# Transposing the heads' outputs on VectorE and placing the squares with 16 on-chip transfers a tile

## The reference

```python
qkv = shift_token(x) @ wqkv                    # 8 heads of 64
q, k, v = (to_heads(t) for t in jnp.split(qkv, 3, axis=-1))
q, k = rotary_xpos(l2norm(q) * qs, l2norm(k) * ksc)
o = local_attention(q, k, v)                   # windows of 64, looking one window back
o = o.transpose(0, 2, 1, 3).reshape(b, n, INNER)   # INNER = 512
x = x + o @ wo
a, g = jnp.split(layernorm(shift_token(x)) @ w1 + b1, 2, axis=-1)
x = x + (a * gelu(g)) @ w2 + b2
```

## Time and profile before

| | |
|---|---|
| median of three runs | 3070.92 us |
| the profiled execution | 3069.8 us |
| its span in the profile | 3068.0 us |
| TensorE (PE) busy | 2989.9 us, 97% |
| VectorE (DVE) busy | 2589.6 us, 84% |
| ScalarE (ACT) busy | 2090.5 us, 68% |
| GpSimd (POOL) busy | 1746.9 us, 57% |
| DMA packets of the hardware queue | 311106 |

### The profile page before, as it was taken

How to read it: one execution, slowest core, us unless ns; L and a number is a source line. 1 busy time by engine, 2 the same in 40 slices (tenths; PEclk the granted TensorE clock), 3 DMA queues, 4 the chain that set the end, 5 groups by cost and what they waited for, 6 DMA issues and landing times.

```text
span 3068.0 us, 84550 instructions
## 1 busy us (share of the span) xinstructions
PE 2989.9 (97%) x30773; PEld 2157.2 (70%) x30773; DVE 2589.6 (84%) x5526; ACT 2090.5 (68%) x5016; POOL 1746.9 (57%) x1158
## 2 busy tenths in 40 slices
PE   7999999999999999989999699999999999999999
PEld 4777777667777777657777477777766677777765
DVE  7999998678888888869999599999966888888866
ACT  4777777437777777328889377777753677777732
POOL 8888886125666665540000588888721566666610
PEclk8999999999999999999999799999999999999999
DMA  5222222202222232100000122222320122222221
GB/s 131 50 51 51 50 59 60 48 16 48 49 52 50 51 65 57 41 1 1 1 1 1 24 52 50 53 50 52 70 48 19 42 49 53 50 49 59 57 49 42
DMA packets 311515, 138.26 MB, mean 45 GB/s; under 512 B 225897, under 2 KB 276546, under 8 KB 311106
## 3 DMA queue, kind: packets, MB, share of 16 engines
q1 hardware_dynamic: 311106, 132.84, 19.8%
HBM read 28.13 MB, written 19.66 MB: 16 GB/s over the span
## 4 chain that ended last, share of the span: by engine, by line
PE 90%; DVE 4%; issue 2%; POOL 2%; ACT 1%; SPq 0%; DMA 0%; DVEq 0%; ACTq 0%; POOLq 0%
PE psum L1264 14%; PE psum L1139 11%; PE psum L1238 7%; PE psum L1281 7%; PE psum L1312 7%; PE psum L1292 7%; PE psum L1194 6%; PE psum L1165 5%; PE psum L1226 5%; PE psum L1522 3%; PE psum L1326 3%; PE psum L1339 3%; PE psum L1498 3%; PE psum L1184 3%; PE psum L1508 2%
## 5 line engine op out<-in xcount | busy, mean ns | idle before, releaser
L491 POOL TENSOR_TENSOR rnorm<-ssq_floor,neg_half 128x16 f32<-128x16 f32 x256 | 750.4, 2931 | 499.7 <-DVE qkr L813 494.9
L566 ACT ACTIVATE shared<-psum,neg_max 128x128 f32<-128x128 f32 x2048 | 595.2, 396 | 40.5 <-DVE neg_max L789 40.5
L496 POOL TENSOR_TENSOR qk_cos<-qk_cos,qk_sin 128x1024 f32<-128x1024 f32 x256 | 607.3, 2372 | 0.0
L1264 PE MATMUL psum<-wqkv,hT 128*128 128x512 f32 x1024 | 533.6, 605 | 15.2 <-DVE qk_sin L775 8.5
L587 ACT COPY shared<-psum 128x512 f32<-128x512 f32 x256 | 150.1, 586 | 438.2 <-PE psum L1226 438.2
L775 DVE TENSOR_TENSOR qk_sin<-psum,sin 128x512 f32<-128x512 f32 x512 | 350.5, 685 | 101.8 <-ACT sq L573 100.9
L780 DVE TENSOR_TENSOR qk_cos<-psum,cos 128x512 f32<-128x512 f32 x512 | 350.6, 685 | 80.0 <-ACT sq L573 79.8
L625 ACT ACTIVATE shared<-psum,b1g 128x512 f32<-128x512 f32 (+1 forms) x192 | 131.6, 686 | 353.8 <-PE psum L1139 350.7
L573 ACT ACTIVATE sq<-psum 128x512 f32<-128x512 f32 x512 | 334.2, 653 | 25.3 <-PE psum L1264 25.3
L1139 PE MATMUL psum<-shared,w1g 128*128 128x512 f32 (+1 forms) x768 | 345.6, 593 | 5.4 <-DVE shared L879 4.0
L1292 PEld LDWEIGHTS psum<-wo,shared 128*128 128x128 f32 x2048 | 267.6, 191 | 115.6 <-issue 114.9
(11 more groups left out here) (132 smaller groups left out, 6373.5 us busy)
## 6 DMA issues: line engine op xcount, KB each, us to landing
vprev<-v SPq DMA_DIRECT2D x512, 130.0 KB, 2.3
token_blocks<-blocks SPq DMA_DIRECT2D x236, 64.0 KB, 1.6
hT<-token_blocks SPq DMA_DIRECT2D x944, 16.0 KB, 1.8
shared<-Y SPq DMA_DIRECT2D x32, 256.0 KB
shared<-Y SPq DMA_DIRECT2D x32, 224.0 KB
out<-X SPq DMA_DIRECT2D x8, 512.0 KB, 3.2
X<-in_L_attn_x SPq DMA_DIRECT2D x7, 512.0 KB, 6.7
wqkv<-in_L_ffn_wqkv SPq DMA_DIRECT2D x4, 512.0 KB, 3.6
```

What stands on the lines that cost most here:

```text
L491: nc.gpsimd.tensor_tensor(rnorm[:], ssq_floor[:], neg_half[:], ALU.pow).then_inc(rnorm_ready, 1)
L496: nc.gpsimd.tensor_tensor(both, both, qk_sin[:, t.m % 2, :], ALU.add).then_inc(sum_ready, 1)
L566: last = nc.scalar.activation(probs[:, c * P:(c + 1) * P], bank(3 + i, (c % 4) * P, (c % 4 + 1) * P), ACT.Exp, bias=neg_max[:, c:c + 1])
L1264: nc.tensor.matmul(bank(i), hT[:, t.m * P:(t.m + 1) * P], wqkv[:, i * INNER:(i + 1) * INNER], start=True, stop=True).then_inc(qk_psum, 1)
```

## The change

Tiles 0 to 57 of a layer (`by_dma`) take a new way for the heads' outputs; the last six (`LAST = 6`) keep the way over TensorE and ScalarE.

- VectorE transposes o of tile s - 1 in squares of 32 (`heads_blocks`, one instruction of 128x512) in the slot in which it is written, into one of two buffers `head_blocks`.
- SP issues 16 transfers for the tile (`place_heads`), each moving four squares of 32x32 from on-chip memory to on-chip memory, into one of four buffers `o_T`. They stand in SP's slot behind the store and the four loads, and ahead of the two copies of v.
- `project_out` and `add_heads` of these tiles run one slot later (tile s - 3) and read `o_T`. TensorE's four transposes and ScalarE's copy go away for them.
- The weighted values lie in banks 6 and 7, so that maxima, sums and shares are one VectorE instruction each over both banks.

```diff
+LAST = 6
...
+        head_blocks = shared[:, 8 * N:9 * N].rearrange("p (q n) -> p q n", q=2)
+        o_T = [shared[:, lo:lo + INNER] for lo in (9 * N, 9 * N + INNER, 3 * N, 3 * N + INNER)]
...
+        def by_dma(t):
+            return t.row < NT - LAST
...
+            def place_heads(t):
+                k = dma_count(t)
+                sp.wait_ge(head_blocks_ready, k + 1)
+                wait(sp, attn_ready, NT * t.L + max(t.row - 3, 0))
+                for j in range(P // SQUARE):
+                    for b in range(P // SQUARE):
+                        to = o_T[k % 4][j * SQUARE:(j + 1) * SQUARE, :].rearrange("i (c n) -> i c n", n=P)
+                        sp.dma_start(to[:, :, b * SQUARE:(b + 1) * SQUARE],
+                                     head_blocks[b * SQUARE:(b + 1) * SQUARE, k % 2, j * P:(j + 1) * P]
+                                     .rearrange("i (c n) -> i c n", n=SQUARE)).then_inc(heads_in[k % 4], 16)
...
                 if t := late_tile(L, s + 5):
                     load_blocks(t)
+                if (t := tile_at(L, s - 1)) and by_dma(t):
+                    place_heads(t)
...
             def exponents(t, i):
-                act.wait_ge(max_ready, 2 * t.n + i + 1)
+                act.wait_ge(max_ready, t.n + 1)
...
+                nc.vector.tensor_reduce(neg_max[:], scored, AX_X, ALU.max, negate=True).then_inc(max_ready, 1)
...
+            def heads_blocks(t):
+                k = dma_count(t)
+                dve.wait_ge(o_ready, t.n + 1)
+                if k > 1:
+                    dve.wait_ge(heads_in[(k - 2) % 4], 256 * ((k - 2) // 4 + 1))
...
+                nc.vector.transpose(head_blocks[:, k % 2, :].rearrange("p (j c n) -> p j c n", j=4, c=4),
+                                    o.rearrange("p (c j n) -> p j c n", c=4, j=4)).then_inc(head_blocks_ready, 1)
...
             def project_out(t):

-                wait(pe, oT_ready, before(t, 0))
+                if by_dma(t):
+                    k = dma_count(t)
+                    pe.wait_ge(heads_in[k % 4], 256 * (k // 4 + 1))
+                    squares = o_T[k % 4].rearrange("p (c n) -> p c n", c=INNER // P)
+                else:
+                    pe.wait_ge(oT_ready, last_count(t) + 1)
...
                     weigh_values(tile(-1))
-                    if t := tile(-2):
-                        heads_transpose(t)
...
-                    if t := tile(-2):
+                    if t := tile(-3):
                         project_out(t)
```

More of the change, by code:

```diff
@@ L630, in local_slot @@
                     tokens(t)
-                tail = s >= NT - 4
                 if s == NT:
                     gated(group_at(L, 0), 0)
-                if not tail and (t := tile_at(L, s - 2)):
-                    outputs(t)
                 if t := tile_at(L, s):
                     exponents(t, 0)
-                if tail and (t := tile_at(L, s - 2)):
+                if (t := tile_at(L, s - 2)) and not by_dma(t):
                     outputs(t)
@@ L784, in maxima @@
             def maxima(t):
[L785 to L790, removed]
+                scored = psum[:, 3 * BANK:5 * BANK].rearrange("p (h k) -> p h k", k=P)
@@ L792, in sums @@
+                wait(dve, scores_ready, before(t, 0))
+                wait(dve, probs_ready, before(t, 1, 2))
+                nc.vector.tensor_reduce(neg_max[:], scored, AX_X, ALU.max, negate=True).then_inc(max_ready, 1)
             def sums(t):
                 wait(dve, pv_ready, before(t, 0))
[L794 to L797, removed]
+                wait(dve, o_ready, before(t, 1))
@@ L799, in shares @@
+                nc.vector.reciprocal(rsum[:].rearrange("p (i h) -> p i h", i=2),
+                                     weighted()[:, :, :, DH]).then_inc(rsum_ready, 1)
             def shares(t):
[L800 to L807, removed]
+                dve.wait_ge(rsum_ready, t.n + 1)
@@ new lines, in shares @@
+                if u := tile_at(t.L, t.row - 1):
+                    if by_dma(u):
+                        dve.wait_ge(head_blocks_ready, dma_count(u) + 1)
+                    else:
+                        dve.wait_ge(oT_psum, last_count(u) + 1)
+                elif t.L:
+                    dve.wait_ge(oT_psum, LAST * t.L)
+                nc.vector.tensor_tensor(
+                    o.rearrange("p (i h d) -> p i h d", i=2, d=DH), weighted()[:, :, :, 0:DH],
+                    rsum[:].rearrange("p (i h) -> p i h", i=2).unsqueeze(3).to_broadcast([P, 2, 4, DH]),
+                    ALU.mult).then_inc(o_ready, 1)
@@ new lines, in heads_blocks @@
+            def heads_blocks(t):
[3 more added lines that the diff above has]
+                    dve.wait_ge(heads_in[(k - 2) % 4], 256 * ((k - 2) // 4 + 1))
+                if t.row == 0 and t.L == DEPTH:
+                    dve.wait_ge(out_psum, NT)
+                elif t.row == 0:
+                    wait(dve, mlp_ready, NG * t.L)
+                nc.vector.transpose(head_blocks[:, k % 2, :].rearrange("p (j c n) -> p j c n", j=4, c=4),
+                                    o.rearrange("p (c j n) -> p j c n", c=4, j=4)).then_inc(head_blocks_ready, 1)
@@ L936, in local_slot @@
                     shares(t)
+                    if by_dma(t):
+                        heads_blocks(t)
                 if t := tile_at(L, s + 4):
                     queries(t)
-                if t := tile_at(L, s - 2):
+                if (t := tile_at(L, s - 3)) and by_dma(t):
+                    add_heads(t)
+                if (t := tile_at(L, s - 2)) and not by_dma(t):
                     add_heads(t)
@@ L1135, in gates @@
                     pe.wait_ge(hid_ready, 3 * t.n + c + 1 - lag)
-                if t.row == 1 and c == 1:
+                if t.row == 1 and c == 0:
+                    pe.wait_ge(hid_ready, 3 * t.n - 1)
+                elif t.row == 1 and c == 1:
                     pe.wait_ge(x1_ready, NT * (t.L + 1))
@@ L1272, in project_v @@
                     wait(pe, rot_ready, 4 * (t.n + 1) + 2)
-                elif u := tile_at(t.L, t.row - 5):
-                    wait(pe, oT_ready, before(u, 0))
+                elif u := tile_at(t.L, t.row - 2):
+                    wait(pe, qT_ready, before(u, 0))
                 else:
@@ L1376, in local_slot @@
                     weights_transpose(tile(0), 0)
+                    if by_dma(tile(-3)):
+                        project_out(tile(-3))
                     project_out(tile(-2))
```

38 lines of the change are left out of this document (25 added, 13 removed).

## The result

The changed kernel takes 4690.97 us in the median of four runs (4684.19 to 4692.09), the kernel before 3069.48 us: a ratio of 1.528, interval 1.5261 to 1.5300. It is slower, as forecast, but by 1621 us and not by 648: the range of 3460 to 4015 us doesn't hold it.

What follows compares the result with a forecast made beforehand. The prediction took SP's queue to become the bound: 3.43 + 7.5 = 10.9 us a slot where PE needs 7.59, so +162 us a layer, +648 over four, 3069.8 + 648 = 3718 us; range 3460 to 4015 (8 in 10).

Steps and rivals of the forecast that it cites:

- 0.69 us estimated: VectorE: the new 128x512 transpose takes 0.69 us alone, 0.6 us back to back.
- 8.3 and 7.7: VectorE's slot after the change: 8.3 us where layer statistics are also due, 7.7 us elsewhere.
- rival 1: SP's queue: issues are cheap, under 0.26 us, VectorE sets the slot; 77 us less, 2993 us; chance 0.03.
- the prediction's own 7.85 us: VectorE: its mean slot after the change, about 7.85 us, said to hide more than half of TensorE's gain.
- TensorE's 0.59 us a slot: TensorE: four transposes a tile go away for 58 tiles, slot becomes 7.59 us, at most 137 us of gain.
- I take 0.47 us each: SP's queue: each of the sixteen new issues priced like the token-block loads, 7.5 us a slot in all.
- rival 2: SP's queue: on-chip transfers cost what the present on-chip copies do, 0.58 us an issue; 4133 us; chance 0.13.
- the prediction's own sum: SP's time per layer: 57 periods, last sixteen, landing 1.8, w2/b2 loads 1.8, token loads 9.9; 644.6 us, +162.
- what SP does already per slot: SP's queue: store to first load 0.44, four loads 1.84, two copies 1.15, together 3.43 us a slot.
- the last six tiles: End of each layer: edits cost nothing, hidden behind PE; uncovered, each would cost 0.7 us once a layer.
- the line that projects the heads' outputs: TensorE: this line would wait about 3 us in each slot for the sixteen transfers.
- Rival 3: TensorE: its clock falls in new gaps; at a lasting 0.66 its slot is 11.5 us, total 3850; chance 0.07.

Runs made afterwards that it cites:

- e1: Changed kernel with 4 transfers of 128 rows in place of 16 of 32 rows, same bytes and packets, squares landing in wrong places: 3041.87 us, ratio 0.9907.
- e7: Changed kernel with its sixteen on-chip transfers in runs of 512 bytes, 32 pieces each in place of 128: 4631.43 us.
- e3: Changed kernel with the squares stored to HBM by one transfer and fetched one slot later by sixteen loads: 4177.22 us, ratio 1.361.
- e4: Changed kernel with the two copies of v issued ahead of the sixteen transfers: 4668.65 us.
- e5: Changed kernel with the squares sent by way of HBM, one scattering store and four loads a tile, output complete: 3060.09 us, ratio 0.9971.
- e6: Changed kernel by way of HBM with one store and four loads, in runs of 512 bytes, VectorE and TensorE using a stride of four numbers: 3192.74 us, ratio 1.0397.
- e8: Changed kernel with eight of the sixteen transfers issued by ScalarE at the end of its slot, eight by SP: 3650.46 us, ratio 1.1892.

## Why the prediction missed

*Right: the mechanism.* SP's queue became the bound through the number of its issues (chain, e1, e7), and the engines that move the data did not (21.6%).

*Right: the other engines.* VectorE's new transpose takes 711 ns against 0.69 us estimated, and the slots without SP's limit are 8.31 and 7.71 us against 8.3 and 7.7 (that VectorE alone sets them is not shown). e1 brings rival 1's case about by fewer issues and not by cheap ones: the gain shows, but 27 us of it, not 77. One slip stands beside it: by the prediction's own 7.85 us, VectorE leaves 0.33 of TensorE's 0.59 us a slot, so it would hide less than half of the gain, not more.

*Wrong: the price, "I take 0.47 us each ... because their shape and run length are those of the new transfers".* The number of pieces and the run length hardly matter (e1, e7); a source on chip in place of one in HBM does (e3). Sixteen issues take 10.35 us; the steps between them are 0.644 us. The trace of before had the row, the second copy at 597 ns; rival 2 took the mean with the first copy, which looks cheap because nothing stands ahead of it (467 ns, against 516 behind a load in e4 and 599 behind an on-chip transfer). Even rival 2's 0.58 us, 4133 us, was too low. By the prediction's own sum 0.644 us gives 57 x (3.43 + 10.3) + 10.3 + 13.5 = 806.4 us a layer, +324 and not +162: 4365 us.

*Wrong: "what SP does already per slot ... 3.43".* Those durations were of a queue with idle time. In the full queue the first copy takes 599 ns and not 467, the store 530 and not 344: 0.32 us a slot. Another 0.23 us lies in gaps and small differences: 0.10 us behind the loads and behind the last copy where the sum has 0.04, 0.03 in the loads and 0.08 in the sixteen. So the clean round of 14.28 us is 0.55 over the 13.73 of the sum, in 57 x 4 rounds 125 us.

*Missed: long issues.* Away from the token loads, the rounds last 14.9 to 15.1 us in a layer's mean, 0.7 over the clean 14.28, in 228 rounds some 165 us. Of the 5639 issues in the trace 230 take over 0.85 us; what they take over the median of their line adds up to 161 us. In 85% of them a packet of one of the instruction queues (q8, q14) starts from 0.6 us ahead of the issue to its end; of the other issues 14% have one in a stretch of 1.5 us. The 230 hold the 32 third token loads, which take 926 ns in the median by themselves; of the other 198 it is 95%. The store at 613.75 is such a one; the loads behind it are not. The DMA queues in these two stretches, 613.7 to 615.7 and 615.7 to 617.6:

```profile
q1 hardware_dynamic: 147, 0.24, 54.2%
q14 instruction: 1, 0.01, 2.0%
...
q1 hardware_dynamic: 437, 0.11, 25.1%
```

The 54.2% are no sign of a cause, since the copies of v land ahead of every store: the engines are 61% busy around the 15 long stores and 60% around the others. That the fetching of instructions holds an issue up is a correlation; no experiment here tests it. Before the change 96 issues took over 0.85 us, 32 of them third token loads, and the steady slots stayed at 8.18 us, so SP's idle time covered them. With these, 4365 + 125 + 165 = 4655 us.

*Wrong: "the last six tiles ... I cost their edits at nothing".* From the last v projection of a layer to the next layer's first (or the end) the changed kernel takes 5.8, 2.9, 7.3 and 5.8 us more than the kernel before, 22 us: there both ways of placing the outputs meet, and which edit costs this is not shown. That makes 4677; 14 us are not accounted for.

*Wrong: who waits.* I named the line that projects the heads' outputs. It was the q and k projection, queued behind the sixteen by way of its loads.

*Rival 3, the clock.* It fell to 0.83 in the stretch, as its condition said, but PE was busy only 78.55 of 120 us: it stayed hidden behind SP.

*The range.* It let the price run from 0.40 to 0.55 us and left out the row at 0.60, and nothing in it stood for what a queue loses when it has no idle time left.

*The Trainium skill.* The rule weighed in the prediction (the Trainium skill, "DMA: Bandwidth & Descriptors", anatomy of one DMA: a dispatch of some 50 ns, small costs for making descriptors) is written of transfers issued from GpSimd, and none here is. Of SP's issues the second half holds, pieces are nearly free (from 32 to 512 of them the issue goes from 591 to 640 ns, e7 and e1); but the fixed part on SP is twelve times the dispatch that the page names.

## What to carry to other kernels

A DMA queue is an engine: before adding transfers, add up what its issues take in a slot, with the rows measured back to back, and compare the sum with the slot of the bound engine. In this kernel many small transfers were a question of how many are asked for, not of bytes or pieces; let one transfer do more of the addressing, even over HBM (4 loads and a store instead of 16 on-chip transfers turned 1.528 into 0.997), and give some to another engine with room (0.991, and 0.987 with the token loads spread as well). When a resource goes from half idle to full, price its old work again as well, and leave room for its disturbances.

## What the chip showed that was not expected

- The same transfer costs SP 432 ns to issue when it comes from HBM and 601 ns when it comes from on-chip memory, and landing takes 1.8 us in both.
- A store of 2048 pieces returns after 435 ns, and the issue behind it takes 956 ns; behind a store in whole rows it takes 467 (e5 against e3 and e6).
- ScalarE's and SP's issues go on side by side at their full price each: SP's take 602 ns and took 601 alone, ScalarE's 628 beside one of SP's and 622 in the 22 cases almost without (e8).
- A stride of 16 bytes makes VectorE's transpose take 1125 ns and not 711, and TensorE's weight load 329 ns and not 192 (medians, e6).
